# Attention on one core: VectorE turns the last query tile's probabilities in blocks of every fourth column, one store and one load put them in place

## What is computed

```python
q = jnp.einsum('ahe,bce->bach', W_Q, x)
k = jnp.einsum('ahe,bce->bach', W_K, x)
v = jnp.einsum('ahe,bce->bach', W_V, x)
scores = jnp.einsum('bach,baCh->bacC', k, q)
masked = jnp.where(causal, scores, jnp.float32(-MASK_VAL))
attn = jax.nn.softmax(masked / np.float32(np.sqrt(D_HEAD)), axis=-1)
z = jnp.einsum('bacC,baCh->bach', attn, v)
out = jnp.einsum('aeh,bach->bce', W_O, z)
x = x + out
```

## Time and profile before

| | us |
|---|---|
| median of 3 runs | 969.71 (969.61 to 970.89) |
| span of the profiled execution | 970.0 |
| before the attention stage | 181.4 |
| attention stage, 63 step lengths | 624.0 |
| after it | 164.6 |

### The profile page before, as it was taken

How to read it: one execution, slowest core, us unless ns; L and a number is a source line. 1 busy time by engine, 2 the same in 40 slices (tenths; PEclk the granted TensorE clock), 3 DMA queues, 4 the chain that set the end, 5 groups by cost and what they waited for, 6 DMA issues and landing times.

```text
span 970.0 us, 24404 instructions
## 1 busy us (share of the span) xinstructions
PE 934.5 (96%) x7618; PEld 793.2 (82%) x7618; DVE 783.1 (81%) x3083; ACT 717.5 (74%) x2040; POOL 280.6 (29%) x328
## 2 busy tenths in 40 slices
PE   7899999899999999999999999999999999999994
PEld 6789999778787887878777787878778786999994
DVE  7878879688797788789789878978978987886666
ACT  3777667587878778787877878777877867787881
POOL 5777003322021012312221321310100111657551
PEclk9999999999999999999999999999999999999998
DMA  9678565121122122121112122111111113557757
GB/s 250 204 221 259 168 168 164 41 49 35 39 51 56 34 54 54 42 45 40 47 38 45 40 40 46 35 53 26 48 31 30 41 53 99 162 153 214 218 163 212
DMA packets 95935, 91.30 MB, mean 94 GB/s; under 512 B 30288, under 2 KB 71536, under 8 KB 95808
## 3 DMA queue, kind: packets, MB, share of 16 engines
q1 hardware_dynamic: 82896, 69.45, 25.7%
q0 software_dynamic: 8352, 18.17, 7.2%
q10 hardware_dynamic: 4560, 2.12, 0.8%
HBM read 64.50 MB, written 25.20 MB: 92 GB/s over the span
## 4 chain that ended last, share of the span: by engine, by line
PE 83%; DMA 4%; DVE 4%; issue 3%; POOL 2%; ACT 2%; SPq 1%; POOLq 0%; DVEq 0%; ACTq 0%
PE psum L2484 15%; PE psum L2473 14%; PE psum L2430 13%; PE psum L2315 9%; PE psum L2492 7%; PE psum L2266 7%; PE psum L2267 7%; PE psum L2268 7%; POOL x_slots L799 2%; PE psum L2278 1%; PE psum L2154 1%; PE psum L2288 1%; ACT arena L1073 1%; DMA arena<-x_slots 1%; DMA y_rows<-y_sb,y_tok 1%
## 5 line engine op out<-in xcount | busy, mean ns | idle before, releaser
L1073 ACT ACTIVATE arena<-arena,neg_max 128x512 f32<-128x512 f32 (+3 forms) x512 | 281.1, 556 | 1.6 <-DVE neg_max L1900 1.6
L1900 DVE CUSTOM_DVE_ANT_0 arena<-psum,causal 128x512 f32<-128x512 f32 (+3 forms) x512 | 217.2, 482 | 3.0 <-PE psum L2430 3.0
L1081 ACT ACTIVATE arena<-psum 128x512 f32<-128x512 f32 x192 | 107.8, 596 | 140.6 <-PE psum L2473 140.6
L2484 PE MATMUL psum<-arena 128*64 128x512 f32 (+3 forms) x1024 | 152.0, 439 | 0.7 <-DVE arena L1913 0.7
L2473 PE MATMUL psum<-ident,arena 128*128 128x128 f32 x1280 | 150.5, 273 | 1.1 <-ACT arena L1073 0.7
L1016 ACT ACTIVATE arena<-psum,b_t 128x256 f32<-128x256 f32 (+1 forms) x336 | 120.9, 444 | 35.6 <-PE psum L2268 26.5
L818 POOL DMA_INDIRECT arena<-y_tiles,y_at x64 | 61.2, 956 | 290.8 <-PE psum L2430 207.1
L2473 PEld LDWEIGHTS psum<-ident,arena 128*128 128x128 f32 x1280 | 141.9, 141 | 1.7 <-ACT arena L1073 1.1
L2315 PE MATMUL psum<-w_sb,arena 128*128 x1136 | 140.8, 275 | 0.4 <-DVE y_sb L1770 0.3
L2484 PEld LDWEIGHTS psum<-arena 128*64 128x64 f32 x1024 | 68.0, 136 | 83.9 <-issue 74.1
L799 POOL DMA_INDIRECT x_slots<-xr,slot x64 | 62.1, 970 | 252.8 <-PE psum L2430 206.9
(11 more groups left out here) (358 smaller groups left out, 1897.4 us busy)
## 6 DMA issues: line engine op xcount, KB each, us to landing
arena<-inv_dram SPq DMA_DIRECT2D x128, 128.0 KB, 2.9
w_raw<-in_L_ffn_W_dram SPq DMA_DIRECT2D x60, 256.0 KB
xg<-x_slots SPq DMA_DIRECT2D x43, 144.0 KB
arena<-in_L_ffn_W_dram SPq DMA_DIRECT2D x24, 256.0 KB
arena<-y_rows SPq DMA_DIRECT2D x16, 256.0 KB, 4.7
y_tiles<-y_sb SPq DMA_DIRECT2D x27, 128.0 KB, 2.2
x_slots<-blank SPq DMA_DIRECT2D x18, 144.0 KB
arena<-x_slots SPq DMA_DIRECT2D x15, 144.0 KB
```

The costliest lines, as they stand in the source:

```text
L1073: ins = act.activation(prob_tile(i, h, t), prob_tile(i, h, t), ACT.Exp, scale=-1.0, bias=neg_max[i % 2][:, h, t:t + 1], accum_out=row_sum[ ...
L1081: act.activation(four_turned(g), turned_bank(i, g), ACT.Copy).then_inc(pt_act, 1)
L1900: ins = dve.tensor_tensor_reduce(out=prob_tile(i, h, t), in0=score_tile(t, h), in1=causal[:, SEQ - (t + 1) * P:SEQ], scale=-1.0, scalar=-2 ...
L2484: ins = pe.matmul(RING_C[m, k * P:SEQ], v_sb[i // V_PAIRS % 2][:, k, col:col + DH], probs_t[:, h * 10 * P + PT_COL[k]:h * 10 * P + PT_COL[ ...
```

## The change

In all steps but the last, the last query tile's squares (t = 3, four per head, eight in all) are no longer turned by TensorE.

- VectorE, `turn_long(i)`: behind its maxima of step i it transposes both heads' 512-wide rows of tile 3 with two instructions, which turn each block of 32 x 32 within its 32 partitions. The columns of a block are every fourth column of the row (`p (k r j) -> p k j r`). The result lies in `turned`, 1024 columns.
- SyncE's queue, `turn_long(i)`, ahead of `spread_sums(i)`: one store of 512 KB to DRAM (each partition's 4 KB in one piece), a wait until it has landed, a wait for `attend(i-1)`, one load of 512 KB back into `late_t` (1 KB pieces), which lies in the last four slots of `y_sb` (now `y_all`).
- TensorE: `transposes` has 12 squares in three groups; k, q and v follow, q without a wait for ScalarE; `attend` first does the columns of tiles 0 to 2, then waits for the load (`late_loaded`) and does tile 3's 128 columns, four products for each head.
- ScalarE: the exponentials of tile 3 go ahead of `transposed(i-1)`, which still has three copies.
- VectorE: `invert(i-1)` goes ahead of `maxima(i, 0, [3])`; the two copies L1913 are gone.
- The last step keeps its 20 transposes and five copies. Some constants' semaphores are merged into `const_ready`, with the same waits.

```diff
     R = 2
+    BLOCK = 32
     TS = R * P
...
         xh = [sb(f"xh{i}", [D, P]) for i in range(2)]
-        y_sb = [sb(f"y_sb{i}", [P, R, D]) for i in range(YRING)]
+        y_all = sb("y_all", [P, YRING * R * D])
+        y_sb = [y_all[:, i * R * D:(i + 1) * R * D].rearrange("p (r d) -> p r d", r=R) for i in range(YRING)]
...
         P_COL = [0, P, 3 * P, 6 * P]
-        PT_COL = [0, 4 * P, 7 * P, 9 * P]
+        PT_COL = [0, 3 * P, 5 * P]
         probs = [[lot(10 * P) for h in range(2)] for i in range(2)]
         probs_t = lot(20 * P)
+        turned = probs_t[:, 12 * P:20 * P]
+        EACH = 2 * QT * BLOCK
+        LATE_IN = range(YRING - P // BLOCK * EACH // (R * D), YRING)
+        late_t = y_all[:, LATE_IN.start * R * D:]
         v_sb = [lot(QT * 4 * P).rearrange("p (k m) -> p k m", k=QT) for i in range(2)]
...
         inv_dram = nc.dram_tensor("inv_dram", [2, 2, P, QT], fp32).ap()
+        turned_dram = nc.dram_tensor("turned_dram", [2, P // BLOCK, P, EACH], fp32).ap()
...
                 return (RING_B, RING_A, RING_C, RING_B, RING_A)[g]
-            return (RING_C, LONG[0], LONG[1], K_BANK if i == STEPS - 2 else Q_BANK, RING_C)[g]
+            return (RING_C, *LONG)[g]
...
             return probs_t[:, g * 4 * P:(g + 1) * 4 * P]
+        def stored_long(steps):
+            return 16 * steps
+        def long_block(h):
+            return turned.rearrange("p (j h k s) -> p h k j s", h=2, k=QT, s=BLOCK)[:, h]
+        def late_square(i, h, k):
+            if i == STEPS - 1:
+                return turned[:, (h * QT + k) * P:(h * QT + k + 1) * P]
+            return late_t.rearrange("p (g h k s) -> p h k g s", h=2, k=QT, s=BLOCK)[:, h, k]
...
+            def turn_long(i):
+                par = i % 2
+                sp.wait_ge(turned_ready, i + 1)
+                wait(sp, late_loaded, 16 * (i - 1))
+                sp.dma_start(turned_dram[par].rearrange("g (p j) e -> (g p) (j e)", j=P // BLOCK), turned).then_inc(turned_stored, 16)
+                sp.wait_ge(turned_stored, stored_long(i + 1))
+                if i == 0:
+                    for j in LATE_IN:
+                        sp.wait_ge(y_stored[j], stored(last_in_place(j, NTS[0])))
+                wait(sp, z_ps, i)
+                sp.dma_start(late_t.rearrange("p (g e) -> p g e", e=EACH), turned_dram[par].rearrange("g p e -> p g e")).then_inc(late_loaded, 16)
             load_first_tiles()
...
             for i in range(STEPS):
+                if i < STEPS - 1:
+                    turn_long(i)
                 spread_sums(i)
...
                 wait(act, z_ps, i)
-                for g in (0, 2, 3):
+                for g in (0, 1, 2) if i < STEPS - 1 else (0, 2, 3):
                     act.wait_ge(pt_ps, PT_USES * i + g + 1)
+                    if g == 3:
+                        act.wait_ge(turned_stored, stored_long(STEPS - 1))
                     act.activation(four_turned(g), turned_bank(i, g), ACT.Copy).then_inc(pt_act, 1)
...
                         high_w(1, 0)
+                    exps(i, 0, [3])
                     if i > 0:
...
                         high_x(1, 0)
-                    exps(i, 0, [3])
                     if i + 1 < STEPS:
...
-            def transposed(i, g):
+            def turn_long(i):
+                dve.wait_ge(exp_done, S_USES * i + 1)
+                wait(dve, turned_stored, stored_long(i))
+                for h in range(2):
+                    ins = dve.transpose(long_block(h), prob_tile(i, h, QT - 1).rearrange("p (k r j) -> p k j r", k=QT, r=BLOCK))
+                ins.then_inc(turned_ready, 1)
+            def last_transposed(g):
+                i = STEPS - 1
                 dve.wait_ge(pt_ps, PT_USES * i + g + 1)
                 wait(dve, z_ps, i)
+                if g == 4:
+                    dve.wait_ge(turned_stored, stored_long(i))
                 dve.tensor_copy(four_turned(g), turned_bank(i, g)).then_inc(pt_dve, 1)
...
                     b, s = divmod(i, PAIRS)
-                    maxima(i, 0, [3])
                     if i > 0:
                         invert(i - 1)
+                    maxima(i, 0, [3])
                     maxima(i, 1, [2])
                     maxima(i, 2, [1, 0])
-                    if i > 0:
-                        transposed(i - 1, 1)
-                        transposed(i - 1, 4)
+                    if i < STEPS - 1:
+                        turn_long(i)
                     if s == (1 if b > 0 else 2):
...
                 invert(STEPS - 1)
-                transposed(STEPS - 1, 1)
+                last_transposed(1)
                 finish(work)
-                transposed(STEPS - 1, 4)
+                last_transposed(4)
                 finish(seek_tiles(1))
...
-                squares = [(h, k, t) for h in range(2) for k in range(QT) for t in range(k, QT)]
-                for g in range(5):
+                squares = [(h, k, t) for h in range(2) for k in range(QT - 1) for t in range(k, QT - 1)]
+                if i == STEPS - 1:
+                    squares += [(h, k, QT - 1) for h in range(2) for k in range(QT)]
+                for g in range(len(squares) // 4):
                     if i < STEPS - 1:
...
                             pe.wait_ge(max_ready, S_USES * (i + 1) + 1)
-                        if g == 3:
-                            pe.wait_ge(max_ready, S_USES * (i + 1) + 2)
-                        if g == 4:
-                            pe.wait_ge(pt_act, PT_ACT * i + 1)
                     else:
...
                         if g == 4:
-                            pe.wait_ge(pt_dve, PT_DVE * i + 1)
+                            pe.wait_ge(pt_dve, 1)
                     for n, (h, k, t) in enumerate(squares[4 * g:4 * g + 4]):
...
                 pe.wait_ge(pt_act, PT_ACT * (i + 1))
-                pe.wait_ge(pt_dve, PT_DVE * (i + 1))
+                def value(k, h):
+                    col = i % V_PAIRS * P + h * DH
+                    return v_sb[i // V_PAIRS % 2][:, k, col:col + DH]
+                for k in range(QT - 1):
+                    for h in range(2):
+                        m = slice(h * DH, (h + 1) * DH)
+                        pe.matmul(RING_C[m, k * P:(QT - 1) * P], value(k, h),
+                                  probs_t[:, h * 6 * P + PT_COL[k]:h * 6 * P + PT_COL[k] + (QT - 1 - k) * P], start=(k == 0), stop=False)
+                if i == STEPS - 1:
+                    pe.wait_ge(pt_dve, 2)
+                else:
+                    pe.wait_ge(late_loaded, 16 * (i + 1))
                 for k in range(QT):
...
                         m = slice(h * DH, (h + 1) * DH)
-                        col = i % V_PAIRS * P + h * DH
-                        ins = pe.matmul(RING_C[m, k * P:SEQ], v_sb[i // V_PAIRS % 2][:, k, col:col + DH],
-                                        probs_t[:, h * 10 * P + PT_COL[k]:h * 10 * P + PT_COL[k] + SEQ - k * P], start=(k == 0), stop=(k == QT - 1))
+                        ins = pe.matmul(RING_C[m, (QT - 1) * P:SEQ], value(k, h), late_square(i, h, k), start=False, stop=(k == QT - 1))
                 ins.then_inc(z_ps, 1)
...
                         project_k(i + 1)
+                        project_q(i + 1)
                     pe.wait_ge(max_ready, S_USES * (i + 1))
...
                         project_v(i + QT - 1, RING_B)
-                    if i + 1 < STEPS:
-                        wait(pe, pt_act, PT_ACT * i)
-                        project_q(i + 1)
-                    else:
+                    if i + 1 == STEPS:
                         transpose_x(1, 0)
```

32 lines of the change are left out of this document (17 added, 15 removed).

## The result

The changed kernel takes 986.35 us (982.73 to 988.02, 4 runs), the kernel before 970.06 (969.61 to 970.89, 4 runs). The ratio is 1.0152, 95% interval 1.0136 to 1.0169: 1.5% slower, where 957 had been forecast. The time lies in the range, but on the other side of no change. Of the profiled execution (span 983.6 against 970.0: 13.6 us more, where the medians of the runs differ by 16.3), 1.0 us more stands ahead of the attention stage, 6.2 in it and 6.4 behind it.

The account below looks back on a forecast made before the run. TensorE was taken to set the 9.97 us step; longest engine 9.56, plus 0.1 handing over and 0.1 queue, gives 9.76; 0.21 saved in 62 steps is 13.0, so 970.0 becomes 957 us, range 936 to 1003 (own range 948 to 966).

Parts of the forecast that it names:

- the queue's ring: SyncE's stream waits twice a step for a landing; round put at 9.15 us a step, it just fits.
- SyncE's queue: Prediction's part on the two 512 KB transfers a step, 3.55 us each; load hidden with 3 us to spare.
- charge of 0.1 us: On SyncE's queue, 0.1 us a step for collisions with GpSimd's DMAs.
- handing over: Between VectorE and the other engines, now without slack: 0.1 us a step; also included in the 9.15 us round of SyncE's queue.
- Rival 2: SyncE's queue bounds: GpSimd's DMAs delay the sums' store by 1.2 us, 10.35 us in some 48 steps; 985 us, chance 0.22.
- that sign: On SyncE's queue, distance from a store of squares to the next load: 3.6 us if the forecast is right.
- rivals 1 and 3: VectorE transposes: free 16-byte step, 0.70 us each, 941 us, chance 0.15; or dear, 2.14 each, 1054 us, chance 0.10.
- rival 4: TensorE's narrow attention products run one head after the other, back at 9.97 us a step; 971 us, chance 0.11.
- The engines' sum: Longest of TensorE, ScalarE and VectorE in each step of the attention stage, mean 9.56 us.
- the sign for a light step: Steps with little VectorE side work should take 9.2 us and show ScalarE waiting 1.4 us for the maxima.

Follow-up runs that it names:

- the first: Changed kernel with the 4 KB reciprocals' store issued ahead of the 512 KB load on SyncE's queue: 1003.26 us where the kernel before takes 1031.29, ratio 0.9731.
- the second: Changed kernel without store and load of the turned squares and all waits on them, tile 3's probabilities left out: 1000.07 us, ratio 0.9680 to the kernel before.
- half-load experiment: Changed kernel with only 256 KB of the turned squares loaded back, half of the late squares left out: ratio 0.9833 to the kernel before.

## Why the prediction was wrong

**The step that failed** is the queue's ring, in the part "SyncE's queue" and in its charge of 0.1 us, and in the ring one term: the 3.75 us from the load's issue to the landing of the sums' store. Its terms, as priced and as the mean over the rounds of steps 8 to 55 shows them:

| term | priced | measured |
|---|---|---|
| load to first spreading load | 3.75 | 4.84 |
| first spreading load to the landing of the next squares' store | 5.20 | 5.24 (1.39 to the store, 3.85 from it to the load) |
| handing over | 0.20 | in the above |
| ring | 9.15 | 10.09 |

The mechanism was seen ("the 4 KB store of sums lands only behind the load"), and the size was not. The load was given 3.55 us where the earlier trace rows had 4.3 for 512 KB and the slope from other sizes was believed instead; it landed in 4.3. The fixed part of that slope, 1.75 us, came from a store (`y_tiles<-y_sb`, 128 KB in 2.2); from the 128 KB load of the same rows, 2.9, and 1.36 for the other 384 KB at 290 GB/s, the estimate would have been 4.26. The small store, issued 0.53 us after the load, then took 4.31 to be landed and acted on; I had let it land with the load. Together 1.09 us, less the 0.20 that was charged for handing over, and they turn a ring that "just fits" under 9.76 into one above 9.97. That this waiting was the cause, and not the traffic or the transposes, is what the first, the second and the half-load experiment show. The Trainium skill (DMA: Bandwidth & Descriptors, Queues, rings and completion order) has a DMA's semaphore count only after every earlier write of the same DMA engine; the trace agrees, 4.2 us in the median for 4 KB behind a load against 2.7 in the earlier trace rows.

**What it cost.** The forecast of 957.0 misses the profiled 983.6 by 26.6 us. In the 48 middle steps 10.04 instead of 9.76 make 13.5. In the last seven, 73.3 us where 69.9 less 7 x 0.21 had been forecast, 4.9. Behind the stage 6.4, which had no term at all: there the last squares' store, load and products follow each other in the open. The rest, 1.8, is ahead of the stage and in its first eight steps. Against the median of the runs, 986.35, the miss is 29.4; the 2.8 us more than in the profiled span are not divided here.

**The 0.1 us** charged for the queue had the same fault in small. It was a mean over steps, but the ring, once it is the longer one, is paid in full in each of them: the first and the last step of a batch, 9.23 and 8.90 by the sum of the engines, take 9.41 and 10.10 in the windows above. No run varied it alone.

**Rival 2** named the right place and 985 us, for another reason, so that its time came out is luck. It had GpSimd's DMAs delay the small store. The trace does not bear that out: from reciprocals' store to spreading load the median is 4.22 us where GpSimd's packets fell into it (49 steps) and 4.31 where none did (14 steps); and with half the load, GpSimd's DMAs as they were, it fell by 1.0.

**What held.** The squares are turned 7.8 us into a step in the median (7.9 forecast), and the next load goes out 3.6 us behind their store in the median, as forecast: that sign alone would not have given the miss away. The transposes: 1.07 forecast from L1919, 1.09 measured, which ends rivals 1 and 3. The Trainium skill (SBUF — State Buffer, Door 1: The DMA port swizzle) lets fp32 be strided for free up to four elements; 1.09 against 0.69 us disagrees, and its sentence that a line of 16 bytes wants two hits is the one that fits. Attention's narrow products: in one step the 28 passes take from 666.13 to 668.45, when the next scores start, 2.32 us. By the same measure the 16 passes of the earlier trace rows take 2.31 (254.83 to 257.14; the row itself says 2.38), so rival 4 is out. TensorE's busy time fell by 0.72 of the 0.84 us a step. The engines' sum: 9.56 and 0.1 for handing over forecast 9.66, and 9.51 is what they need with the queue out of the way. VectorE's busy time in the second to fifth step of a batch was put at 10.02, 9.78, 9.43 and 9.70 and in batch 5 is 9.56, 9.82, 9.31 and 10.15. ScalarE waits for the maxima, 157.2 us in 63 times in the stage, 2.5 each where 1.4 had been named as the sign for a light step. The load is hidden: TensorE stood 3.1 us for it in five instructions. At step 60 the table loads stand ahead of the next squares' store; it takes 12.5 us where it took 10.8.

## What to carry to other kernels

A queue that waits for a landing is an engine: add its waits up round once, and compare the sum with the shortest step, not with the mean. Put a small store that is waited for ahead of a large load in the same queue, not behind it, but see first that its data are ready early, since now it holds up the rest. When steps are longer than any engine is busy and idle times read "issue", look at the queue's own timeline, and compare the start of the idle engine's instruction with the landing of the DMA that it reads.

## What was not expected of the hardware

The 16 KB packets of kind "instruction", by which the engines' instructions are fetched (41 in the stage, 0.88 to 1.76 us each), go together with longer transfers beside them. Where none ran later than 1 us after its issue, the squares' store took 3.57 us to the load's issue (median, 41 steps; 3.60 in 7 more with GpSimd's packets); where one did, 4.73 (11 steps), and 5.05 with GpSimd's packets besides (4 steps). That the packet holds up the store's share on its DMA engine is the likely reason, and not shown. For the load the sign is weaker: it landed in 4.57 us where such a packet fell into it (22 steps) and 4.11 where none did (41 steps), but single ones without a packet took up to 5.6. One load in the trace with a packet, and one without, by the windows 661.3 to 666.4 and 441.0 to 446.5:

```profile
q8 instruction: 1, 0.02, 2.2%
...
y_all<-turned_dram SPq DMA_DIRECT2D x1, 512.0 KB, 5.5
inv_dram<-inv_sum SPq DMA_DIRECT2D x1, 4.0 KB, 5.3
```
```profile
y_all<-turned_dram SPq DMA_DIRECT2D x1, 512.0 KB, 4.0
...
inv_dram<-inv_sum SPq DMA_DIRECT2D x1, 4.0 KB, 3.4
```

Fifteen such stores at 1.1 to 1.5 us each are some 19 us of waiting in the stage, an estimate and an upper bound, since not every step has the queue on its path. No run took the packets away, so their share in the loss is not shown. The Trainium skill (Runtime: NRT & Kernel Launch, Instruction fetch mechanics) gives 16 KiB blocks and calls their cost mostly hidden; the longer stores above are on the side of a cost to the transfers beside them, which no run here isolates.

A step in the write cost VectorE about what a step in the read did: 0.37 us for 512 fp32 written in steps of 512 bytes (the maxima), 0.40 for 512 read in steps of 16 bytes (the transposes).
